# Twelve experts' low parts moved into the first stage of a layer kernel, and its first steps, fetches, routing and joint put in another order

## The reference: what is computed

```
xn = layernorm(x)
scores = (xn w_q)(xn w_k)^T / 8, causal; attn = softmax(scores) (xn w_v1 w_v2)
logits = xn w_router^T; e = argmax(logits); s = sigmoid(logits[e])
routed = (up * silu(gate)) down_proj[e],  [gate, up] = (s xn) gate_up_proj[e]
shared = (silu(xn w_gate^T) * (xn w_up^T)) w_down^T
out = x + attn + routed + shared
```

## Time and profile before

| what | value |
|---|---|
| time, median of 3 runs | 242.66 us (242.14 to 243.34) |
| the profiled execution's own time | 243.21 us |
| its span, first to last instruction | 239.9 us |
| PE busy | 211.4 us, 88% of the span |
| PE weight load | 183.3 us, 76% |
| DVE busy | 155.7 us, 65% |
| ACT busy | 130.6 us, 54% |
| POOL busy | 110.8 us, 46% |

### The profile page before, as it was taken

How to read it: one execution, slowest core, us unless ns; L and a number is a source line. 1 busy time by engine, 2 the same in 40 slices (tenths; PEclk the granted TensorE clock), 3 DMA queues, 4 the chain that set the end, 5 groups by cost and what they waited for, 6 DMA issues and landing times.

```text
span 239.9 us, 4858 instructions
## 1 busy us (share of the span) xinstructions
PE 211.4 (88%) x1399; PEld 183.3 (76%) x1401; DVE 155.7 (65%) x396; ACT 130.6 (54%) x329; POOL 110.8 (46%) x130
## 2 busy tenths in 40 slices
PE   4695999999996669999992899999999999899993
PEld 4484887898775559979881679998898897798792
DVE  3946887867748667678769466996665666405501
ACT  2354688678452566675674245554444444655741
POOL 1903030300001767777796006665665666738700
PEclk9997999999999999999998599999999999999999
DMA  6999999900000631541460113233233220019731
GB/s 174 398 361 337 190 172 303 256 23 0 0 4 1 176 99 55 146 132 48 103 172 0 47 44 87 78 85 80 85 84 87 81 77 19 3 45 290 237 87 44
DMA packets 30004, 28.26 MB, mean 118 GB/s; under 512 B 2563, under 2 KB 27146, under 8 KB 29344
## 3 DMA queue, kind: packets, MB, share of 16 engines
q1 hardware_dynamic: 27456, 23.77, 38.0%
q0 software_dynamic: 2528, 4.24, 5.6%
HBM read 14.28 MB, written 10.50 MB: 103 GB/s over the span
## 4 chain that ended last, share of the span: by engine, by line
PE 76%; DVE 12%; issue 5%; ACT 3%; DMA 1%; POOL 1%; DVEq 0%; ACTq 0%
PE acc L1163 13%; PE acc L1237 9%; PE big L1004 8%; PE big L1006 7%; PE big L1005 7%; PE mid L1147 6%; PE acc L1061 6%; PE mid L1226 4%; PE big L1134 4%; PE big L1131 4%; PE mid L1114 2%; DVE wel L732 2%; PE mid L1034 2%; PE acc L1025 1%; DVE stats L454 1%
## 5 line engine op out<-in xcount | busy, mean ns | idle before, releaser
L429 POOL DMA_INDIRECT y_rows<-y,ids x47 | 46.0, 978 | 36.7 <-ACT y L966 19.3
L419 POOL DMA_INDIRECT scratch<-rows,slot x32 | 32.3, 1009 | 41.3 <-DVE slot L651 30.7
L1163 PE MATMUL acc<-vr_all,pt 128*128 128x128 f32 x288 | 40.3, 277 | 0.6 <-ACT pt L912 0.3
L1163 PEld LDWEIGHTS acc<-vr_all,pt 128*128 128x128 f32 x288 | 36.5, 191 | 2.0 <-issue 1.1
L690 DVE TENSOR_REDUCE negmax<-big 128x1 f32<-128x128 f32 (+7 forms) x32 | 24.0, 755 | 21.2 <-PE big L1134 20.9
L905 ACT ACTIVATE prob<-big,negmax 128x128 f32<-128x128 f32 (+7 forms) x32 | 23.8, 744 | 19.6 <-DVE negmax L690 19.4
L912 ACT COPY pt<-mid 128x512 f32<-128x512 f32 (+3 forms) x48 | 22.8, 476 | 13.5 <-PE mid L1147 13.0
L774 DVE COPY eht<-mid 128x512 f32<-128x512 f32 (+1 forms) x24 | 16.3, 680 | 21.2 <-PE mid L1226 21.2
L966 ACT COPY y<-acc 128x256 f32<-128x256 f32 (+1 forms) x24 | 8.8, 368 | 34.0 <-PE acc L1237 34.0
L1237 PEld LDWEIGHTS acc<-wed,eht 128*128 128x128 f32 x188 | 24.5, 191 | 3.7 <-issue 1.9
L1147 PE MATMUL mid<-identf,prob 128*128 128x128 f32 x144 | 23.8, 274 | 3.3 <-ACT prob L905 2.7
(11 more groups left out here) (128 smaller groups left out, 439.2 us busy)
## 6 DMA issues: line engine op xcount, KB each, us to landing
we_raw<-w_gate_up SPq DMA_DIRECT2D x4, 1024.0 KB, 11.8
scratch<-blank SPq DMA_DIRECT2D x1, 3120.0 KB, 25.3
xe<-scratch SPq DMA_DIRECT2D x24, 130.0 KB
wed<-w_down SPq DMA_DIRECT2D x1, 2048.0 KB, 30.4
q_raw<-qk_all SPq DMA_DIRECT2D x8, 256.0 KB, 4.9
k_raw<-qk_all SPq DMA_DIRECT2D x8, 256.0 KB, 5.2
expert_out<-y_rows SPq DMA_DIRECT2D x8, 256.0 KB, 4.9
out<-res SPq DMA_DIRECT2D x8, 256.0 KB, 3.8
```

The costliest lines, as they stand in the source:

```text
L419: pool.indirect_dma_start(scratch, bass.IndirectOffsetOnAxis(ap=slot[:, t:t + 1], axis=0), rows[:, t, :], None).then_inc(row_sent[t % FLY] ...
L429: pool.indirect_dma_start(y_rows, bass.IndirectOffsetOnAxis(ap=ids[:, t:t + 1], axis=0), y[p % NY][:, t % 2, :], None, bounds_check=NT * P ...
L1163: last = pe.matmul(acc[g][:, cols], pt[n % 2][:, cols], v, start=kb == 0 and r == 0, stop=True, skip_group_check=True)
```

## The change

1. POOL makes the low parts of experts 0 to 11 (`IN_STAGE`) in the first stage, three in a row behind the normalised rows of each of groups 4 to 7 (`weights_beside`). Experts 12 to 15 are made in eighths (128x64, `PARTS`), one behind each of the 32 row transfers. DVE makes none.
2. The opening is written in another order: DVE finishes all statistics of batch entry 1 ahead of `xt_lo(1)`, POOL fills its constants earlier, PE makes 28 instead of 12 warm-up transposes.
3. SP fetches x of entries 2 and 3 earlier, and the last quarter of the expert weights, the blank rows and w_down behind the first copy of queries and keys.
4. Both halves of the split of queries and keys of entry 0 are made in steps 5 and 6 (before: in step 6, step 7 and the joint). ACT rounds experts 9 to 15 later (`HIGH_FROM`), 14 and 15 in the joint.
5. Routing: `choose`, `sum_tiles`, `place_experts` and `place_tokens` come ahead of the last two `hidden`, `rank` ahead of the last half of `gate_up`. The last hidden tiles have their own place (`h_last`), so that they don't wait for `down(6)`.
6. The first four score tiles of entry 0 have a PSUM half each (`score_block`), and wait for no exponentials; `exp` of tile 3 no longer waits for the shared part. `name_experts` moves from entry 0 to entry 1.

The diff, cut to its core:

```
+PARTS = 8
+IN_STAGE = 12
+HIGH_FROM = (0, 3, 6, 9, 10, 12, 14)
...
+            def weights_lo(e, part=0, parts=1):
+                cols = slice(part * 2 * FE // parts, (part + 1) * 2 * FE // parts)
                 pool.wait_ge(weh_ready, e + 1)
...
+            def weights_beside(g):
+                pool.wait_ge(xn_ready[g % 2], (g // 2 + 1) * GT)
+                n = IN_STAGE // 4
+                for e in range((g - GT) * n, (g - GT + 1) * n):
+                    weights_lo(e)
             for b in range(1, B):
                 for u in range(2):
                     rsqrt(b, u)
+                if b == B - 2:
+                    weights_beside(2 * B - 4)
+                    weights_beside(2 * B - 3)
+            weights_beside(2 * B - 2)
+            weights_beside(2 * B - 1)
...
                 pool.indirect_dma_start(scratch, bass.IndirectOffsetOnAxis(ap=slot[:, t:t + 1], axis=0),
                                         rows[:, t, :], None).then_inc(row_sent[t % FLY], 16)
-            for e in range(ON_DVE, NE):
-                weights_lo(e)
+                weights_lo(IN_STAGE + t // PARTS, t % PARTS, PARTS)
...
             xt_lo(0)
-            dve.wait_ge(const_made, CONSTS)
             dve.wait_ge(x_loaded[1], 16)
-            statistics(1, range(BT // 2))
+            statistics(1, range(BT))
+            for part in (statistics_2, statistics_3, statistics_4, statistics_5):
+                part(1)
             xt_lo(1)
             top_logit(0)
-            statistics(1, range(BT // 2, BT))
-            for part in (statistics_2, statistics_3, statistics_4, statistics_5):
-                part(1)
+            normalize(2)
             hidden(0, 0)
...
+                    if g == NG - 3:
+                        split_k(0, 0)
+                        split_q_lo(0, 0)
...
+            for part in range(4):
+                choose(B - 1, part)
             sum_tiles(0)
+            sum_tiles(1)
             hidden(NG - 2, 0)
-            sum_tiles(1)
+            place_experts()
             hidden(NG - 2, 1)
+            place_tokens()
             to_score(NG - 1)
             hidden(NG - 1, 0)
-            place_experts()
             hidden(NG - 1, 1)
...
-                    for k in range(PER_BATCH if b < B - 1 else 0):
-                        weights_lo(PER_BATCH * (b - 1) + k)
+                if b == 1:
+                    name_experts()
```

More of the change, by code:

```diff
@@ L141, in build @@
         wsl = sb("wsl", [P, DOWN0 - QK0], F32R)
+        xth_at = top[0]
         a, a_end = overlay(top[0], [(f"xth{n}", [P, GC], F32R) for n in range(XB)]
@@ L278, in _, with load_weights @@
             sp.dma_start(ws_raw[:, :], w_small).then_inc(ws_loaded, 16)
[L279 to L282, removed]
+            def load_weights(b):
                 e = slice(b * EB, (b + 1) * EB)
                 sp.dma_start(we_raw[:, e, :], w_gate_up[:, e, :]).then_inc(we_loaded[b], 16)
[L286 to L289, removed]
+            load_x(1)
+            for b in range(B - 1):
+                if b < B - 2:
+                    load_x(b + 2)
+                load_weights(b)
             def load_raw(col):
@@ L378, in _ @@
             rsqrt(0, 1)
[L379 to L386, removed]
+            pool.wait_ge(xtl_ready[0], 1)
             pool.wait_ge(const_step, 6)
@@ L715, in first_half @@
                         if i == 1:
-                            place_tokens()
-                            split_k(0, 1)
-                            split_q_lo(0, 1)
-                        if i == 2:
+                            add_shared(NG - 3)
+                        if i == 4:
+                            add_shared(NG - 2)
                             add_shared(NG - 1)
@@ L853, in step @@
                 score_tanh(g)
-                for e in range(3 * (g - 2), min(3 * (g - 1), NE)):
+                for e in range(HIGH_FROM[g - 2], HIGH_FROM[g - 1]):
                     weights_hi(e)
-                if g == NG - 2:
+                if g == NG - 3:
                     split_q_hi(0, 0)
+                    split_q_hi(0, 1)
                 gate(g - 1, 0)
@@ L884, in _ @@
             keep_qk(0)
+            gate(0, 0)
             score_tanh(0)
             keep_logits(1)
[L887 removed]
             keep_qk(1)
+            keep_xt(2)
             score_tanh(1)
[L890 removed]
             gate(0, 1)
@@ L915, in first_half @@
                 if first:
-                    for i in range(3):
+                    for i in range(GT):
                         exp(b, i)
-                    for u in range(2):
-                        act.wait_ge(shared_added[u], FIRST + B)
-                    exp(b, 3)
                     keep_pt(b, 0)
@@ L925, in first_half @@
                     exp(b, BT - 1)
+                    for e in range(HIGH_FROM[-1], NE):
+                        weights_hi(e)
                 else:
@@ L1102, in rank @@
                           ).then_inc(ranked, 1)
+            count()
             gate_up(NG - 1, 0)
-            count()
+            rank()
             gate_up(NG - 1, 1)
-            down(NG - 2)
-            rank()
             def transpose_rows(p, q):
@@ L1168, in first_half @@
                 if first:
-                    for i in range(GT):
+                    for i in range(GT + 1):
                         scores(b, i)
                         if i == 1:
-                            down(NG - 1)
-                    scores(b, GT)
+                            down(NG - 2)
+                    down(NG - 1)
                     pe.wait_ge(ranks_used, 1)
@@ L1178, in first_half @@
                     scores(b, BT - 1)
+                if first:
+                    scores(b, GT + 1)
                 for n in range(GT):
-                    if first and n + 1 < GT:
-                        scores(b, GT + n + 1)
+                    if first and n < 2:
+                        scores(b, GT + n + 2)
+                    if first and n == GT - 1:
+                        weigh(b, n)
+                        transposes(b, n + 1)
+                        continue
                     if not (b == B - 2 and n == GT - 1):
```

96 lines of the change are left out of this document (52 added, 44 removed).

## The result

The changed kernel takes 235.74 us (median of 4 runs, 235.72 to 236.03) against 242.72 (4 runs, 242.14 to 243.34) in the same session: ratio 0.9719, 95% interval 0.9683 to 0.9755. The forecast was 235.1 with a range of 231.0 to 239.5. The profiled execution took 235.74, its span is 233.7. The span became 6.2 us shorter and the time 7.5 (243.21 before), so 1.3 us of that pair lies outside the spans, and I compare places inside the spans only.

A forecast was written before the change was run, and what follows sets the result against it. PE's longest wait, 5.1 us at the expert stage's entry, and the half clock there were taken as the main bound. Opening -6.3, steps 3 to 6 +6.35, joint and entry -7.6 gave -7.6 from 242.66: 235.1 us, range 231 to 239.5.

The forecast's parts named there:

- The opening: Start of the kernel: earlier statistics and full clock bring `project_x(2)` to 17.9 instead of 24.24, 6.3 us gained.
- Steps 3 to 6: First stage: POOL's runs of three low parts hold DVE to their end, and splits delay hidden tiles; 6.35 us lost.
- step 3: First stage, a step without splits: 0.3 us lost, or 0.9 with `to_score` held by POOL's low parts.
- Step 4: First stage: `statistics_2` held 2.0 us by POOL's low parts, making PE 1.4 us later.
- The joint: Between first stage and expert stage: earlier routing, fewer waits for exponentials; transposes of 89.55 start at 86.85, 2.7 us earlier.
- The entry: Start of the expert stage: first product at 127.2 instead of 133.67, without half clock; 7.6 us gained.
- I take that it is covered: Row transfers: the idle 0.3 us ahead of each vanishes behind the eighths, so pairs stand about 1.4 us apart.
- rival 2: Expert-stage entry: idle 0.3 us stays, pairs 1.65 us apart, half clock again; entry gains 3.4 us, 239.3 us; 15%.
- rival 3: Row transfers: pairs 1.9 us apart bound the whole, first product 4.4 us later than before, 247.1 us; 10%.
- Rival 1: First stage: DVE hardly held by POOL, only the splits cost, 1.5 + 0.9 us; 231.2 us; 20%.

The follow-up runs named there:

- e7: Changed kernel with DVE's old opening order (second half of entry 1's statistics behind `xt_lo(1)`); 238.37 us, ratio 0.9807 to the kernel before.
- e1: Changed kernel without POOL's twelve low parts in the first stage; 248.86 us, ratio 0.8717, on the chip where the kernel before took 287.74 us.
- the two small kernels: Separate kernels that only copy x out, setting VectorE instructions beside runs of six POOL subtractions; 20 of 29 instructions held, none through the run.
- e5: Changed kernel with experts 12 to 15 made whole behind the row transfers and the splits of attention group 0 moved later; 239.11 us, ratio 0.9867.
- e6: Changed kernel with 12 warm-up transposes in place of 28; 234.5 us, ratio 0.9675 to the kernel before.
- e10: Changed kernel with 14 identity transposes ahead of PE's wait for the first fetched rows and 4 ahead of the second; 233.73 us, ratio 0.9667.
- e11: Changed kernel with 14 and 4 identity transposes at PE's row waits, and attention group 0's splits moved out of steps 5 and 6; 232.48 us, ratio 0.9608.
- e9: The changed kernel once more, without an edit, on the same chip as the runs with filled row waits; 234.42 us, ratio 0.9654.

## Why the prediction came out, point by point

**The time was right with two terms off by 2.6 us each, in opposite directions.** That they cancel is luck, and so is the closeness of 235.1 to 235.74.

- *The opening, -6.3.* `project_x(2)` came at 18.19 instead of 24.04, 5.85 earlier (the 24.24 of the earlier trace rows is its start in the chain that ended last, where the changed kernel has 18.36, 5.88 earlier). Transposes of group 2 came at 15.96 (said 15.5, 15.3 to 15.9), no half clock behind them. Right, within half a microsecond; `e7` shows that the order of VectorE makes 2.8 of it.
- *Steps 3 to 6, +6.35 (lower end 5.0); measured +3.77.* This is the first of two steps that failed: "a DVE operation with two SBUF inputs that comes in this time is held to its end". By `e1`, the splits cost 2.6 us, for which 1.5 + 0.9 was reckoned; the low parts cost 1.26 and not 3.95. VectorE's operations are held for one POOL instruction at a time (1.16, 0.98, 1.27 us), and where VectorE has slack that costs nothing. I had let the two outliers of 4.27 and 1.55 us stand against the rule of the Trainium skill (SBUF — State Buffer, "SBUF: two separate sides"), one whole instruction of lock. In steps 3 to 6, and in the two small kernels, the rule is what the traces show. It made the loss of step 3 its lower end and less (0), as the prediction said it would. In the outliers and in `e5` (5.60 us) it does not hold. Step 4 came out at 1.27 (said 1.4), since two of `statistics_2`'s small operations were held once each, which adds up to nearly the same.
- *The joint, -2.7.* The transposes of 89.55 stand at 84.61; less the 2.17 us by which `down(5)` came earlier, that is 2.77. Slots were ready 8.31 us behind `down(5)`, said 8.0. But the first transfer began 1.03 us behind the slots, where it was 0.31 before. The profile names the score column of the last group (`rows` L544), which VectorE now writes last, 0.07 us behind the slots; what fills the other 0.65 us no row shows, though it is the same in every trace of the new order.
- *The entry, -7.6 with the joint; measured -4.94.* This is the second. From `down(5)`, 2.17 earlier, to the first product, 7.11 earlier, it gained 4.94: 2.77 in the joint and 2.17 behind it. "I take that it is covered" was wrong for the idle time: it shrank from 0.30 to 0.17 us, it did not go. An eighth took 0.33 us (said 0.3). Pairs at 1.58 us in place of 1.4 put the last transfer 31 x 0.18 = 5.6 us later than said, 2.67 us of which PE had to wait for, and the half clock came back, as in rival 2. Rival 2 was the better description of this place.
- *Slower, rival 3.* Far away: it began at 1.75 us for a pair, and 1.58 was measured.

Rival 1's step (hardly held) and rival 2's entry together were never a case of mine. They give -5.94 + 3.77 - 4.94 = -7.1 us at the first product. One late fetch in the middle of the expert stage cost another 1.37 us in this profile (PE waits for `xe` at 168.7; the traces of `before`, `e6`, `e10` and `e11` don't have it there) and is no part of the change.

## What to carry to other kernels

A wait at a stage's entry can absorb a loss upstream or eat a gain: `e6` lost 0.8 us in the opening and nothing in the time. So follow a gain to the next place where engines meet, and ask there what else comes last. When one or two outliers decide a term, look first at how the other instructions of the same pair of engines behaved: here the ordinary case was one instruction's hold, and the outliers were real but rare (three in twelve traces of the big kernel). Cutting a helper's work into small pieces between the instructions of another queue costs a little less than the piece each time (0.25 us for 0.33 here), since the gap ahead of the next transfer shrinks. That makes 8 us on POOL for what takes 5 us whole, and it is cheap against a long run that can hold a neighbour for 5.6 us.

## What was not expected of the hardware

- VectorE beside POOL's subtractions: held to the end of the running POOL instruction also with one input and with 4 columns (1.21 us for 0.16), free with one input in PSUM (0.69 us). Three times held through several POOL instructions, 1.55, 4.27 and 5.60 us.
- In `e6` the transposes at 10.15 ran at half the speed of the changed kernel's, while the granted clock reads 1.00 in that stretch of both. In the opening of these traces the durations tell the clock, not the column.
- At the entry half clock came behind 2.67, 0.79 and 0.47 us of idle PE (changed kernel), behind 1.60, 0.79 and 0.47 (`e9`) and behind 0.72, 1.47 and 0.56 (`e7`), and not behind 1.42, 0.79 and 0.62 (`e6`): the two sides lie close, and no run here says where they part.
- One chip ran the kernel before at 287.74 us. Its stalls fell while the row transfers stood 1.27 us apart, and the kernels with eighths between them took some 249 us there. Whether the spacing is the cause was not tried apart from that.
